# A Perceiver block on one NeuronCore: self-attention's projections placed beside its units, norms batch by batch, biases loaded as columns

## The chip, the cores and the metric

The kernel runs on one NeuronCore of one Trainium2 chip. The metric is the device time of one execution in microseconds (us). Engines: PE is TensorE, DVE is VectorE, ACT is ScalarE, POOL is GpSimd, SP is SyncE, which here only issues DMAs.

## The reference, cut to what matters

Two batches of 256 tokens with 512 features go through three layers. Each layer normalises its input and adds its output to it.

```python
x = x + cross_attention(layernorm(x), ctx)   # 16 heads of 128, 8 key/value heads, 4096 context tokens
n = layernorm(x)                             # self-attention: 16 heads of 32, 256 tokens
Q, K, V = n @ q_w.T + q_b, n @ k_w.T + k_b, n @ v_w.T + v_b
S = K @ Q.T * 32 ** -0.5                     # per batch and head, row i, column j
S = where(i - j < 0, -inf, S) - (i - j)
x = x + (softmax(S) @ V) @ o_w.T + o_b
n = layernorm(x)                             # 8 experts, the best 2 of each token, and a shared one
x = x + routed_experts(n) + 0.2 * shared_expert(n)
```

The projections run in two parts, high and low, of fp32r numbers: each product is three matmuls for each of the four chunks of 128 features, 12 in all for a 128 x 512 result.

## The kernel before, in words

Four stages run one after the other, each a block of five instruction streams (SP, POOL, DVE, ACT, PE) that meet at its end: `queries`, `cross`, `selfattn`, `experts`. A stream is in order. Inside a block semaphores alone order the engines (`wait_ge`, `then_inc`), and the order of the work is written out by hand in each stream. There is no planner. X holds the residual stream, four tiles (TT = 4) of 128 tokens, two (RT = 2) for each batch.

`cross` (L295 to L1119) walks over both batches and 8 key/value heads (a `group` each). In a group PE makes keys and scores into a ring of four PSUM banks (`free`, L986), DVE takes each block of scores out and its maximum (`scores_out`, L823), `maxima` (L830) makes the bias of the exponentials, and ACT computes them (`exp_piece`, L633). The first group of batch 1 (`op` and not `pv`, L926) also adds the last output of batch 0 to X (`residual`, L842) and otherwise makes only keys and scores. In the last group of all, the weights of self-attention are loaded in the order q, k, v, and POOL splits those of q and k (`weight_part`, L116).

`selfattn` (L1122) starts with `ln_vector` (L64) over all four tiles on DVE, with the square root on ACT. PE transposes the result (L1323), ACT copies the high part (L1286), DVE makes the low part (L1214). PE then makes the four chunks of Q and the four of K (L1330); DVE writes Q (L1218), ACT writes K (L1290). Scores of unit 0 follow, then V (L1385), and then the units' loop. A unit n is four heads of one batch: N = 8 units, batch 0 first. In loop n PE issues, in this order: the scores of unit n + 1 (L1340, into the four banks of `s_all`), the transposes of unit n for its first 128 queries (L1353), the values' matmuls of unit n - 1 (L1365), the transposes for the second 128 queries. DVE takes the maxima (`scores`, L1221), makes the reciprocals of the sums (`inverse`, L1234) and copies a part of the turned tiles (`turned`, L1251); ACT does the exponentials (`softmax`, L1292), the other copies (`turned`, L1299) and the high part of the output (`output_high`, L1303); POOL multiplies by the reciprocals (`normalise`, L1197). ACT's order in loop n is softmax(n + 1, 0), turned(n, 0), output_high(n - 1), softmax(n + 1, 1), turned(n, 1). Loop 7 has no scores; in their place stand the output projections of the first two tiles (`out`, L1369), those of batch 1 end the stage. The turned tiles have three PSUM banks, one for each transpose group of a unit.

`experts` (L1405) begins with `ln_vector` (L1602) and the transposes of its result (L1850), which ACT copies twice (L1747, L1748). The biases b1, b2, sb1 are loaded as rows, turned by two transposes (L1853, L1854) and copied by DVE (L1609, L1610). Then come the gate (L1859), the shared expert, whose first layer is L1868, and the eight experts. POOL fills constants, scales a bias (L1576) and adds it to X in one instruction (L1579).

## Time and profile before

| | us |
|---|---|
| median of 3 runs (lowest to highest) | 1970.67 (1969.95 to 1971.15) |
| profiled execution, its own time | 1973.03 |
| its span, first to last instruction | 1971.3 |
| mean granted clock of PE | 0.985 of full |

| share of the span | busy us |
|---|---|
| PE | 1906.8 (97%) |
| DVE | 1094.1 (56%) |
| ACT | 975.7 (49%) |
| POOL | 328.3 (17%) |

The profile is one execution. A line of the timeline is: start in us, duration in us, engine, line of the kernel, operation, output<-inputs, shapes, count of instructions merged into the line, and in brackets the idle time before it and what ended it. A line of the windows' view gives busy us (and instructions) of each engine in a stretch, then the clock granted to PE as a share of full speed, then the DMA engines' share and rate. Self-attention runs from 1418 to 1524 us.

### The profile page before, as it was taken

The page shows a single profiled execution, that of the slowest core. Times are in us where ns is not written, and L with a number is a line of the kernel's source. Part 1 is how long each engine was busy: PE and PEld are TensorE (multiplying, and loading weights), DVE is VectorE, ACT ScalarE, POOL GpSimd, SP SyncE. Part 2 cuts the span into 40 slices and gives each one's busy share as a digit, 9 for nine tenths or more (in the row PEclk, how much of TensorE's full clock was granted, in tenths as well). Part 3 has the DMA queues.
Part 4 walks back from the last instruction along what each step waited for, and adds up shares of the span by engine and source line. Part 5 has one row for each costly group of instructions (what it writes and reads, how often), then busy time and mean ns, then how long its engine had stood idle before and what let it go on. Part 6 is the DMA issues. An engine that isn't in the chain of part 4 may idle for free. (4 is left out here: it accounts for less than half of the span.)

```text
span 1971.3 us, 32041 instructions
## 1 busy us (share of the span) xinstructions
PE 1906.8 (97%) x10480; PEld 1602.1 (81%) x10480; DVE 1094.1 (56%) x2429; ACT 975.7 (49%) x2064; POOL 328.3 (17%) x238
## 2 busy tenths in 40 slices
PE   9999999999999999999999999999787999999998
PEld 6787888888888778878888888887565688999997
DVE  3667677677767666676677677676636531000003
ACT  3204676676577572055775776676526442122111
POOL 0300211211211213011211212211533200000001
PEclk9999999999999999999999999999889899999999
DMA  8651111111111146501111111111300907577552
GB/s 246 214 194 42 43 42 41 51 32 50 45 32 37 43 155 196 173 25 46 36 48 40 37 45 40 37 43 57 104 0 14 352 7 265 203 268 265 198 187 66
DMA packets 123073, 198.12 MB, mean 101 GB/s; under 512 B 12485, under 2 KB 61813, under 8 KB 118896
## 3 DMA queue, kind: packets, MB, share of 16 engines
q1 hardware_dynamic: 119040, 188.59, 28.6%
q10 hardware_dynamic: 2672, 4.55, 0.7%
q0 software_dynamic: 1280, 3.93, 0.6%
q8 instruction: 47, 0.77, 0.2%
q14 instruction: 34, 0.28, 0.0%
HBM read 151.50 MB, written 45.81 MB: 100 GB/s over the span
## 5 line engine op out<-in xcount | busy, mean ns | idle before, releaser
L817 DVE TENSOR_TENSOR crs_ptl<-crs_tp,crs_pth 128x512 fp32r<-128x512 f32 x512 | 352.7, 689 | 178.8 <-ACT crs_pth L650 178.2
L650 ACT ACTIVATE crs_pth<-crs_tp 128x512 fp32r<-128x512 f32 x504 | 301.7, 599 | 245.3 <-PE crs_tp L1036 242.2
L568 POOL TENSOR_TENSOR crs_vl<-crs_vraw,crs_vh 128x512 fp32r<-128x512 f32 x128 | 165.1, 1290 | 1068.8 <-ACT crs_vh L657 1068.7
L1027 PE MATMUL crs_ring<-crs_kh,crs_ql 128*128 128x512 f32 x512 | 233.9, 457 | 0.0
L1046 PE MATMUL crs_ov<-crs_ptl,crs_vh 128*128 128x512 f32 x512 | 210.5, 411 | 10.2 <-DVE crs_ptl L817 8.4
L1046 PE MATMUL crs_ov<-crs_pth,crs_vh 128*128 128x512 f32 x512 | 202.4, 395 | 0.0
L1027 PE MATMUL crs_ring<-crs_kh,crs_qh 128*128 128x512 f32 x512 | 201.5, 394 | 0.0
L1027 PE MATMUL crs_ring<-crs_kl,crs_qh 128*128 128x512 f32 x512 | 200.9, 392 | 0.0
L1046 PE MATMUL crs_ov<-crs_pth,crs_vl 128*128 128x512 f32 x512 | 200.7, 392 | 0.0
L1036 PEld LDWEIGHTS crs_tp<-all_ident,crs_prob 128*128 128x128 f32 x1024 | 142.4, 140 | 69.5 <-ACT crs_more L639 3.7
L639 ACT ACTIVATE crs_prob<-crs_prob,crs_nmax 128x512 f32<-128x512 f32 (+1 forms) x192 | 166.3, 867 | 65.3 <-DVE crs_nmax L832 65.3
L1036 PE MATMUL crs_tp<-all_ident,crs_prob 128*128 128x128 f32 x1024 | 195.2, 272 | 2.8 <-ACT crs_more L639 2.8
L1036 PE MATMUL crs_tp<-all_ident,crs_more 128*128 128x128 f32 x1024 | 195.7, 273 | 0.0
L827 DVE CUSTOM_DVE_ANT_0 crs_more<-crs_ring,crs_maskb 128x512 f32<-128x512 f32 x256 | 172.6, 682 | 0.3 <-issue 0.3
L827 DVE CUSTOM_DVE_ANT_0 crs_prob<-crs_ring,crs_maskb 128x512 f32<-128x512 f32 x256 | 172.6, 683 | 0.0
L639 ACT ACTIVATE crs_more<-crs_more,crs_nmax 128x512 f32<-128x512 f32 (+1 forms) x192 | 166.0, 864 | 0.0
L1721 DVE TENSOR_SCALAR ex_yT<-moe_bank,moe_b_cols 128x160 f32<-128x160 f32 x32 | 10.8, 379 | 273.5 <-PE moe_bank L1992 273.5
L821 DVE TENSOR_TENSOR crs_kl<-crs_ring,crs_kh 128x512 fp32r<-128x512 f32 x128 | 88.4, 691 | 132.5 <-ACT crs_kh L661 132.5
L1808 ACT ACTIVATE ex_hT<-moe_bank,moe_b_cols 128x160 f32<-128x160 f32 x128 | 43.5, 391 | 235.6 <-PE moe_bank L1968 235.6
L1968 PE MATMUL moe_bank<-moe_bufT,moe_w 128*128 128x160 f32 x1024 | 145.4, 302 | 0.7 <-ACT moe_bufT L1803 0.7
L1968 PEld LDWEIGHTS moe_bank<-moe_bufT,moe_w 128*128 128x128 f32 x1024 | 141.5, 192 | 2.8 <-ACT ex_hT L1808 1.0
L1036 PEld LDWEIGHTS crs_tp<-all_ident,crs_more 128*128 128x128 f32 x1024 | 127.6, 140 | 0.0
(279 smaller groups left out, 3334.5 us busy)
## 6 DMA issues: line engine op xcount, KB each, us to landing
moe_w<-in_L_ffn_w SPq DMA_DIRECT2D x48, 1024.0 KB, 12.3
v_scratch<-crs_more SPq DMA_DIRECT2D x64, 512.0 KB, 2.9
crs_vraw<-v_scratch SPq DMA_DIRECT2D x128, 256.0 KB, 2.7
ex_w<-in_L_ffn_w SPq DMA_DIRECT2D x16, 1024.0 KB, 13.4
crs_prob<-in_ctx SPq DMA_DIRECT2D x16, 512.0 KB, 4.7
crs_wo<-in_L_xattn_Wo SPq DMA_DIRECT2D x16, 512.0 KB, 4.1
moe_w<-in_L_ffn_sw SPq DMA_DIRECT2D x8, 1024.0 KB, 12.9
qry_wq<-in_L_xattn_Wq SPq DMA_DIRECT2D x16, 256.0 KB, 3.8
```

What stands on the lines that cost most here:

```text
L568: nc.gpsimd.tensor_tensor(vl[:, n % VR, :, :], vraw[:, :, :], vh[:, n % VR, :, :].bitcast(F32), ALU.subtract).then_inc(s["v_lo"], 1)
L639: act.activation(w, w, ACT.Exp, bias=nmax[:, t:t + 1], accum_out=rs[:, t, PIECE_OF[n]:PIECE_OF[n] + 1]).then_inc(s["p_ready"], 1)
L650: act.activation(pth[:, k % PT, :], tp[k % PT][:, :], ACT.Copy).then_inc(s["pt_hi"], 1)
L817: v.tensor_tensor(ptl[:, k % PT, :], tp[k % PT][:, :], pth[:, k % PT, :].bitcast(F32), ALU.subtract).then_inc(s["pt_lo"], 1)
L821: v.tensor_tensor(kl[:, n % KR, :], ring[k_at(n, op) % RING][:, :], kh[:, n % KR, :].bitcast(F32), ALU.subtract).then_inc(s["ring_free"], 1)
L827: v.tensor_tensor_reduce(probs(t, n * BANK, (n + 1) * BANK), ring[at % RING][:, :], maskb[:, n * BANK:(n + 1) * BANK], op0=ALU.add, op1=AL ...
L1027: m = pe.matmul(ring[at % RING][:, :], a[:, t // RT, rows], w[:, n % KR, :], start=i == 0, stop=i == 2)
L1036: m = pe.transpose(tp[k % PT][:, t * P:(t + 1) * P], probs(t, k * P, (k + 1) * P), ident[:, :])
L1046: m = pe.matmul(ov[:, :], a[:, k // NC % VR, k % NC, :], w[:, k % PT, :], start=k == 0 and i == 0, stop=k == SCH - 1 and i == 2)
L1721: m = v.tensor_scalar(yT[:, c, :], y_ps[c // 2][:, c % 2 * SL:(c % 2 + 1) * SL], b_cols[:, bass.ds(e * KC + c, 1)], None, ALU.add)
L1808: m = act.activation(hT[:, 2 * n + q, :], h_ps[n % 2][:, q * SL:(q + 1) * SL], ACT.Gelu, bias=b1_cols[:, bass.ds(e * FC + (2 * n + q), 1)])
L1968: m = pe.matmul(h_ps[n % 2][:, q * SL:(q + 1) * SL], w1[i][:, c, fc * P:(fc + 1) * P], bufT[:, i, c, :], start=c == 0, stop=c == KC - 1)
```

## The change: what it does

- Layer norm is cut into `ln_variance`, `ln_root`, `ln_deviation` and `ln_scale` for a range of tiles. Statistics and deviation of batch 0 for self-attention are made in the first group of batch 1 of `cross` (on DVE after the residuals of batch 0; the root and two loads of ACT's tables after the keys; the deviation before the last block of scores). Those of batch 0 for the experts are made in the last part of self-attention, after the residuals of batch 0. Batch 1's are made in the stages themselves.
- Self-attention: its weights are loaded and placed in the order v, q, k, so that POOL splits those of v and q in `cross` and those of k in the stage. PE starts with two matmuls on the identity whose result nobody reads, turns batch 0, makes its V, turns batch 1, makes its V, then Q and K of chunk 0 only, and the scores of unit 0. Units alternate between the batches (units 2c and 2c + 1 use chunk c), and the other three chunks of Q and K are made in loops 0 to 4, after the first transposes, the second projection of loop 0 after the second transposes. They use one PSUM bank, `made`; the turned tiles have two banks in place of three, in rotation. DVE writes Q in the loop between the scores and the reciprocal; ACT writes K at the loop's end.
- The first output projection stands after the last unit's transposes, the second after its values.
- Experts: two matmuls on the identity first, transposes batch by batch, POOL's stream waits for the norm before its first fill, and the biases are loaded from arrays turned on the host, without PE and DVE.

```diff
+def ln_variance(v, ch, X, w, start, stop, var_ready):
+    for i in range(start, stop):
+        v.bn_stats(w["stats"][:, i, :], X[:, i, :]).then_inc(ch.sem, 1)
+    ch.n += stop - start
+    v.wait_ge(ch.sem, ch.n)
+    for i in range(start, stop):
+        v.bn_aggr(w["mv"][:, i, :], w["stats"][:, i, :]).then_inc(ch.sem, 1)
+    ch.n += stop - start
+    v.wait_ge(ch.sem, ch.n)
+    v.tensor_scalar(w["veps"][:, start:stop], w["mv"][:, start:stop, 1], EPS, None, ALU.add).then_inc(var_ready, 1)
...
+def ln_deviation(v, ch, w, start, stop, root_ready, count):
+    at = slice(start, stop)
+    v.wait_ge(root_ready, count)
+    ch.link(v.reciprocal(w["div"][:, at], w["root"][:, at]))
+    ch.link(v.tensor_tensor(w["div"][:, at], w["div"][:, at], w["veps"][:, at], ALU.mult))
+    ch.link(v.tensor_tensor(w["div"][:, at], w["div"][:, at], w["root"][:, at], ALU.add))
+    ch.link(v.tensor_scalar(w["div"][:, at], w["div"][:, at], 0.5, None, ALU.mult))
+    ch.link(v.reciprocal(w["rstd"][:, at], w["div"][:, at]))
...
+def ln_scale(v, X, out, w, i, done):
+    m = v.tensor_scalar(out[:, i, :], X[:, i, :], w["mv"][:, i, 0:1], w["rstd"][:, i:i + 1], ALU.subtract, ALU.mult)
+    if done:
+        m.then_inc(done, 1)
...
+                    if op and not pv and n == SB - 3:
+                        act.wait_ge(s["var_ready"], 1)
+                        ln_root(act, norm, 0, RT, s["root_ready"])
+                        act.activation(norm["table"][:, :], ident[:, 0:1], ACT.Exp)
...
+                if op and not pv:
+                    v.wait_ge(s["ring_free"], R + o_at(QT - 1) + 1)
+                    ch = Chain(v, s["ln_chain"])
+                    ln_variance(v, ch, X, norm, 0, RT, s["var_ready"])
...
+                    if op and not pv and n == SB - 2:
+                        ln_deviation(v, ch, norm, 0, RT, s["root_ready"], 1)
...
+    QUERY_BESIDE = {0: 1, 1: 2, 3: 3}
+    KEY_BESIDE = {0: 1, 2: 2, 4: 3}
+    WARM = 2
...
-        bank = [t.ps(f"bank{i}") for i in range(4)]
-        t_ps = (bank[0:1], bank[1:3])
+        turns = [t.ps(f"turn{i}") for i in range(2)]
+        o_bank, made = t.ps("o"), t.ps("made")
+        v_ps = (turns[0], turns[1])
...
+        def t_ps(n, it, j):
+            return turns[(n * BANKS + it + j) % 2]
...
+        def place(n):
+            return n % B * KC + n // B
...
+            def input_low(b):
+                for c in range(KC):
+                    v.wait_ge(s["xT_hi"], b * KC + c + 1)
+                    v.tensor_tensor(xl[:, c, batch(b)], s_all[:, c, batch(b)], xh[:, c, batch(b)].bitcast(F32), ALU.subtract).then_inc(s["xT_lo"], 1)
+            def value(i):
+                v.wait_ge(s["v_ps"], i + 1)
+                v.tensor_tensor(V.rearrange("p (b c) r n -> p b r c n", b=B)[:, i // RT, i % RT], v_ps[i % 2][:, :].rearrange("p (c n) -> p c n", c=KC),
+                                vo_bias[:, 0, :].rearrange("p (c n) -> p c n", c=KC), ALU.add).then_inc(s["v_ok"], 1)
+            def query(c):
+                v.wait_ge(s["q_ps"], c + 1)
+                v.tensor_scalar(qT[:, c, :], made[:, :], bias_cols[:, 0, c:c + 1], HW ** -0.5, ALU.add, ALU.mult).then_inc(s["q_ok"], 1)
+            for i in range(RT):
+                ln_scale(v, X, xn, norm, i, s["xn_ready"] if i == RT - 1 else None)
+            ln_variance(v, ch, X, norm, RT, TT, s["var_ready"])
+            input_low(0)
+            ln_deviation(v, ch, norm, RT, TT, s["root_ready"], 1)
+            for i in range(RT, TT):
+                ln_scale(v, X, xn, norm, i, s["xn_ready"] if i == TT - 1 else None)
+            v.wait_ge(s["vo_ld"], 32)
+            value(0)
+            value(1)
+            input_low(1)
+            value(2)
+            value(3)
             v.wait_ge(s["b_ld"], 32)
-            for c in range(KC):
-                v.wait_ge(s["q_ps"], c + 1)
-                v.tensor_scalar(qT[:, c, :], s_all[:, c, :], bias_cols[:, 0, c:c + 1], HW ** -0.5, ALU.add, ALU.mult).then_inc(s["q_ok"], 1)
+            query(0)
             v.wait_ge(s["consts"], 2)
             def scores(n, it):
...
-                                vo_bias[:, 0, :].rearrange("p (c n) -> p c n", c=KC), ALU.add).then_inc(s["v_ok"], 1)
             for n in range(N):
                 if n < N - 1:
                     scores(n + 1, 0)
+                if n in QUERY_BESIDE:
+                    query(QUERY_BESIDE[n])
                 inverse(n, 1)
...
                     output_low(n - 1)
-            for i in range(RT):
-                residual(i)
+            residual(0)
             output_low(N - 1)
+            residual(1)
+            v.wait_ge(s["out_ok"], RT)
+            ln_variance(v, ch, X, norm_ffn, 0, RT, s["var_ready"])
+            ln_deviation(v, ch, norm_ffn, 0, RT, s["root_ready"], 2)
             for i in range(RT, TT):
...
+            def key(c):
+                act.wait_ge(s["k_ps"], c + 1)
+                act.activation(kT[:, c, :], (made if c else o_bank)[:, :], ACT.Identity, bias=bias_cols[:, 1, c:c + 1]).then_inc(s["k_ok"], 1)
...
+            ln_root(act, norm, RT, TT, s["root_ready"])
+            input_high(1)
+            act.activation(norm["table"][:, :], ident[:, 0:1], ACT.Exp)
             act.wait_ge(s["b_ld"], 32)
-            for c in range(KC):
-                act.wait_ge(s["k_ps"], c + 1)
-                act.activation(kT[:, c, :], bank[c][:, :], ACT.Identity, bias=bias_cols[:, 1, c:c + 1]).then_inc(s["k_ok"], 1)
+            key(0)
...
                     turned(n, it)
                     if n and it == 0:
                         output_high(n - 1)
+                    if it == 1 and n in KEY_BESIDE:
+                        key(KEY_BESIDE[n])
             output_high(N - 1)
+            act.activation(norm_ffn["table"][:, :], ident[:, 0:1], ACT.Sqrt)
+            act.wait_ge(s["var_ready"], 2)
+            ln_root(act, norm_ffn, 0, RT, s["root_ready"])
...
+            def turn_input(b):
+                pe.wait_ge(s["xn_ready"], b + 1)
+                if b:
+                    pe.wait_ge(s["xT_lo"], KC)
+                for c in range(KC):
+                    for i in range(b * RT, (b + 1) * RT):
+                        m = pe.transpose(s_all[:, c, i * P:(i + 1) * P], xn[:, i, c * P:(c + 1) * P], ident[:, :])
+                    m.then_inc(s["xT_ps"], 1)
...
+            def query(c):
+                if c:
+                    pe.wait_ge(s["q_ok"], c)
+                if c > 1:
+                    pe.wait_ge(s["k_ok"], c)
+                project(Q_W, c, made, s["q_ps"])
+            def key(c):
+                if c == 0:
+                    pe.wait_ge(s["w_lo"], 2)
+                else:
+                    pe.wait_ge(s["q_ok"], c + 1)
+                project(K_W, c, made if c else o_bank, s["k_ps"])
             def scores(n, it):
                 if n and it == 0:
...
-                c, b = n % KC, n // KC
+                c, b = n // B, n % B
+                if it == 0:
+                    pe.wait_ge(s["q_ok"], c + 1)
+                    pe.wait_ge(s["k_ok"], c + 1)
...
-                if n:
-                    pe.wait_ge(s["cT_ok"], unit(n - 1, it))
-                    if it == 1:
-                        pe.wait_ge(s["cT2_ok"], n)
                 for j in range(it + 1):
+                    if it + j == 0:
+                        if n:
+                            pe.wait_ge(s["cT_ok"], unit(n - 1, 1))
+                    elif it + j == 1:
+                        if n:
+                            pe.wait_ge(s["cT2_ok"], n)
+                    else:
+                        pe.wait_ge(s["cT_ok"], unit(n, 0))
...
+            for i in range(WARM):
+                pe.matmul(made[:, :].rearrange("p (r n) -> p r n", r=BANK // P), ident[:, :],
+                          ident[:, :].rearrange("p (o n) -> p o n", o=1).to_broadcast([P, BANK // P, P]), start=True, stop=True)
+            turn_input(0)
+            value(0)
+            value(1)
+            turn_input(1)
+            value(2)
+            value(3)
+            query(0)
+            key(0)
+            pe.wait_ge(s["xT_lo"], TT // RT * KC)
             scores(0, 0)
             scores(0, 1)
-            pe.wait_ge(s["w_lo"], 2)
...
             pe.wait_ge(s["v_ok"], TT)
             for n in range(N):
                 for it in range(RT):
-                    if n == N - 1:
-                        out(it)
-                    elif it == 0:
+                    if it == 0 and n < N - 1:
                         scores(n + 1, 0)
                         scores(n + 1, 1)
                     transposes(n, it)
-                    if n and it == 0:
-                        values(n - 1, 0)
-                        values(n - 1, 1)
+                    if it == 0:
+                        if n in QUERY_BESIDE:
+                            query(QUERY_BESIDE[n])
+                        elif n in KEY_BESIDE:
+                            key(KEY_BESIDE[n])
+                        if n:
+                            values(n - 1, 0)
+                            values(n - 1, 1)
+                    elif n in QUERY_BESIDE and n in KEY_BESIDE:
+                        key(KEY_BESIDE[n])
+            out(0)
             values(N - 1, 0)
             values(N - 1, 1)
+            out(1)
             for i in range(RT, TT):
                 out(i)
...
+            pool.wait_ge(s["xn_ready"], B)
             nc.gpsimd.memset(xe[:, :, :, :], 0.0).then_inc(c, 1)
...
-            pool.wait_ge(s["xn_ready"], 1)
...
+            for i in range(RT):
+                ln_scale(v, X, xn, norm, i, s["xn_ready"] if i == RT - 1 else None)
+            ln_variance(v, ch, X, norm, RT, TT, s["var_ready"])
+            ln_deviation(v, ch, norm, RT, TT, s["root_ready"], 1)
+            for i in range(RT, TT):
+                ln_scale(v, X, xn, norm, i, s["xn_ready"] if i == TT - 1 else None)
             for c in range(KC):
...
+            act.activation(norm["table"][:, :], ident[:, 0:1], ACT.Sqrt)
...
+            act.dma_start(b1_cols[:, :], a["L0_ffn_b1"]).then_inc(r, 16)
+            act.dma_start(b_cols[:, 0:SB1], a["L0_ffn_b2"]).then_inc(r, 16)
+            act.dma_start(b_cols[:, SB1:SB1 + FC], a["L0_ffn_sb1"]).then_inc(r, 16)
...
+            ln_root(act, norm, RT, TT, s["root_ready"])
...
+            for i in range(WARM):
+                pe.matmul(bank[7][:, :].rearrange("p (r n) -> p r n", r=BANK // P), ident[:, :],
+                          ident[:, :].rearrange("p (o n) -> p o n", o=1).to_broadcast([P, BANK // P, P]), start=True, stop=True)
+            for b in range(B):
+                pe.wait_ge(s["xn_ready"], b + 1)
+                for c in range(KC):
+                    for i in range(b * RT, (b + 1) * RT):
+                        m = pe.transpose(bank[c][:, i * P:(i + 1) * P], xn[:, i, c * P:(c + 1) * P], ident[:, :])
+                    if b == B - 1:
+                        m.then_inc(s["xT_ps"], 1)
...
+        if name in ("L0_ffn_b1", "L0_ffn_b2", "L0_ffn_sb1"):
+            a = _np.ascontiguousarray(a.reshape(-1, P).T)
```

## Rows read from the trace of the kernel before

**Rows 1.** Windows: stretch and length; PE, PEld, DVE, ACT, POOL busy; PEclk; DMA.
```profile
1418.00:1420.00 2.00, 0.00 (x0) 0.00 (x0) 1.71 (x3) 1.49 (x2) 1.20 (x2) 0.98 0.10 10
1420.00:1422.00 2.00, 0.00 (x0) 0.00 (x0) 1.63 (x9) 0.20 (x1) 0.00 (x0) 0.50 0.80 193
...
1470.00:1472.00 2.00, 0.00 (x0) 0.00 (x0) 1.93 (x10) 1.58 (x9) 1.46 (x1) 0.78 0.00 0
...
1480.00:1500.00 20.00, 14.18 (x215) 9.38 (x215) 17.89 (x93) 19.77 (x78) 10.34 (x9) 1.00 0.01 2
1468.00:1504.60 36.60, 26.12 (x341) 17.77 (x341) 30.17 (x159) 31.97 (x124) 17.13 (x14) 0.91 0.01 2
```

**Rows 2.** Timeline, from the end of cross-attention to the first loop.
```profile
1416.71 0.39 PE L995 MATMUL crs_ring<-crs_woh,crs_pth 128*128 128x512 f32 x1
...
1418.29 2.47 DVE L69 BATCH_NORM_STATS2 att_ln_stats<-all_X 128x6 f32<-128x512 f32 x4 [0.33 <-PEq L358]
...
1422.68 1.92 DVE L85 TENSOR_SCALAR att_xn<-all_X,att_ln_mv,att_ln_rstd 128x512 f32<-128x512 f32 x4
1424.70 3.68 PE L1323 MATMUL att_bank<-all_ident,att_xn 128*128 128x128 f32 x16 [7.60 <-DVEq L1211]
...
1429.79 2.07 PE L1330 MATMUL att_s<-att_xh,all_w_lo 128*128 128x512 f32 x4 [1.41 <-DVE att_xl L1214]
...
1434.41 1.09 PE L1330 MATMUL att_s<-att_xh,all_w_lo 128*128 128x512 f32 x4
...
1455.04 0.94 PE L1340 MATMUL att_s<-att_qT,att_kT 32*128 32x128 f32 x16 [0.87 <-ACT att_kT L1290]
...
1458.74 0.17 DVE L1232 TENSOR_SCALAR att_nmax<-att_mx 128x4 f32<-128x4 f32 x1
...
1468.16 0.94 PE L1340 MATMUL att_s<-att_qT,att_kT 32*128 32x128 f32 x16 [0.78 <-DVE att_V L1261]
```

**Rows 3.** Timeline, one unit of self-attention's loop.
```profile
1484.77 0.94 PE L1340 MATMUL att_s<-att_qT,att_kT 32*128 32x128 f32 x16
...
1487.01 0.64 PE L1365 MATMUL att_bank<-att_cT,att_V 128*32 128x128 f32 x16 [0.36 <-ACT att_cT L1301]
...
1487.15 1.55 POOL L1201 TENSOR_TENSOR att_sc<-att_sc,att_rsum 128x512 f32<-128x512 f32 x1 [1.58 <-DVE att_rsum L1236]
...
1488.75 1.09 PE L1353 MATMUL att_bank<-all_ident,att_sc 128*128 128x128 f32 x8 [1.09 <-POOL att_sc L1201]
...
1489.41 0.51 ACT L1296 ACTIVATE att_sc<-att_sc,att_nmax 128x256 f32<-128x256 f32 x1
...
1489.77 0.94 PE L1340 MATMUL att_s<-att_qT,att_kT 32*128 32x128 f32 x16
...
1491.39 0.57 ACT L1301 ACTIVATE att_cT<-att_bank 128x512 f32<-128x512 f32 x1
```

**Rows 4.** Timeline of PE's weight loads, extra matmuls at the kernel's start.
```profile
8.15 0.19 PEld L271 LDWEIGHTS qry_warm<-all_ident 128*128 128x128 f32 x1 [0.24 <-issue]
8.57 0.19 PEld L271 LDWEIGHTS qry_warm<-all_ident 128*128 128x128 f32 x1 [0.24 <-issue]
```

**Rows 5.** Timeline, last unit of self-attention to the experts' gate.
```profile
1504.60 1.16 PE L1375 MATMUL att_s<-all_w_hi,att_ol 128*128 128x512 f32 x4
...
1524.03 2.47 DVE L69 BATCH_NORM_STATS2 sh_ln_stats<-all_X 128x6 f32<-128x512 f32 x4 [0.32 <-PEq L1131]
...
1535.79 5.37 PE L1859 MATMUL moe_bank<-sh_xnT,moe_gate 128*8 128x512 f32 x8 [1.07 <-ACT sh_xnT L1748]
```

**Rows 6.** Timeline, first group of batch 1 in cross-attention, start and end.
```profile
825.92 2.72 DVE L849 SCALAR_TENSOR_TENSOR all_X<-crs_ring,crs_rinv,all_X 128x512 f32<-128x512 f32 x4
...
829.39 0.69 DVE L821 TENSOR_TENSOR crs_kl<-crs_ring,crs_kh 128x512 fp32r<-128x512 f32 x1 [0.76 <-ACT crs_kh L661]
...
858.44 0.73 ACT L639 ACTIVATE crs_prob<-crs_prob,crs_nmax 128x512 f32<-128x512 f32 x1 [7.85 <-DVE crs_nmax L832]
...
861.42 0.44 PE L1036 MATMUL crs_tp<-all_ident,crs_prob 128*128 128x128 f32 x2 [1.42 <-ACT crs_more L639]
```

124 lines of the change are left out of this document (49 added, 75 removed).

## The prediction

> **What bounds the kernel now.** I read the page first: TensorE (PE) is busy nearly all of the span, so time is lost or won only where PE waits, runs at half clock, or gets more work. Then I cut the span into stretches and looked for PE idle time. From 1400 to 1540 us there is the only long stretch with gaps that the change touches: the end of cross-attention, self-attention and the start of the experts. Behind it PE is full at full clock to the end, so what this stretch gains or loses passes to the end one to one. The small stretches show the granted clock: 0.98 in 1418-1420, though PE's last matmul had ended at 1417.1, 0.50 in 1420-1422; and 0.78 in 1470-1472, in which PE did nothing, three us after the values' projections had kept it full [rows 1, 2]. 0.50 is the lower of the clock's two levels (1.2 GHz), 1.00 the higher (2.4 GHz). Last the timeline, instruction by instruction. At the start of self-attention the norm takes 1418.3 to 1424.7, the transposes of its result run at half clock, eight projections follow, and the first scores come at 1455.04; the values' projection (V) lies behind them, so the units' loop starts with the scores of unit 1 at 1468.16 [rows 2]. A unit then repeats every 5.0 us. Its period is a chain: scores on PE (0.94), the maxima and the reciprocal on DVE (POOL starts 2.38 after the scores), POOL's normalising 1.55, transposes (about 1.0), next scores [rows 3]. ACT is busy 19.77 of 20 us beside it [rows 1]. So the loop is bound by a chain through four engines and by ACT, with PE idle 36.60 - 26.12 = 10.5 us in it [rows 1].
>
> **The change part by part.** I call the stage's start 0 (1418.3) and sum against the profiled execution.
>
> *Start of self-attention.* The statistics of batch 0 are made in cross-attention, so DVE begins with two scalings (0.48 each, a quarter of the old 1.9) and PE has its input at 1.0. PE first runs two extra matmuls, four instructions; at full clock one takes 0.43 (8.15 to 8.57 [rows 4]), so 1.7, and the clock was still full just there [rows 1]. Then 8 transposes: 16 took 3.68 at half clock, so 8 take 0.9 at full; about 1.1 to the first V matmul for ACT's copies (from the end of the old transposes at 1428.4 to the first projection it was 1.4, with twice the columns to copy); V of two tiles. One projection is 2.80: seven from 1434.41 to 1455.04 less 0.9 for the last handover [rows 2]. Then transposes of batch 1 0.9, handover 1.1, V of two tiles, Q0, K0, handover 0.9. Sum: 1.7 + 0.9 + 1.1 + 5.6 + 0.9 + 1.1 + 5.6 + 5.6 + 0.9 = 23.4 to the first scores. DVE's second half of the norm lies beside V0 and V1, POOL's split of the K weights (from about 6.7, 7 long, as before) ends at about 13.7, before K0 at 19.7. Unit 1's scores must wait until DVE has read unit 0's, 3.8 later (1455.04 to 1458.9 [rows 2]); V hid this before, nothing does now. So the loop starts at 27.2 where it started at 49.9: **-22.7**. Six projections (16.8) of that are only moved; 5.9 is norm and half clock.
>
> *Six projections in the units.* Loops 1 and 3 get a query projection, 2 and 4 a key projection, 0 both.
> Query loop: DVE's order is scores of n+1, the query's write, then the reciprocal that POOL waits for. So the chain is scores 0.94, transposes 0.55, Q 2.80, DVE's write with handover 0.95, reciprocal 0.25, POOL 1.6, transposes 0.95: 8.05 in place of 5.0. The projection is wholly on the chain.
> Key loop: the turned tiles now share two banks, so the first transposes of unit n wait for ACT's copy of the unit before (it starts 1.62 and ends 2.19 after the scores: 1491.39 against 1489.77 [rows 3]). Then transposes 0.55 (2.75), K 2.80 (5.55), values 1.0 (6.6; 24 instructions, of which 16 take 0.64 [rows 3]). ACT's queue is in order: its copy of the values' output waits for that, and behind it stand the softmax of the next unit (2.0: 1489.41 to 1491.39), the copy of the turned tile 0.6 and the key's write, 0.7 of the 0.87 that the first scores waited for it [rows 2, 3], for which the next scores wait: 6.6 + 0.5 + 2.0 + 0.6 + 0.7 + handovers 0.3 = 10.7.
> Loop 0: scores, transposes once POOL is done (2.2 after the scores' start), Q 2.8, write and reciprocal 1.2, POOL 1.6, transposes 1.0, K 2.8, write 1.05: 12.65.
> Loops 5 and 6 stay 5.0. Sum 12.65 + 8.05 + 10.7 + 8.05 + 10.7 + 10 = 60.15 against 1504.60 - 1468.16 = 36.4 [rows 2, 5]: **+23.7**. The bounds: PE's 10.5 idle us absorb as much (16.8 - 10.5 = +6.3), or all as above.
>
> *Half clock in the loops.* New gaps on PE: 2.9 before unit 1's scores, 2.8 before loop 0's second transposes, 2.9 at the end of both key loops (while ACT does softmax, copy and key). Both idle stretches of that size in the old trace, at 1418 and at 1470, ended in half clock [rows 1], so I expect most of these to. The first projection before ran 1429.79 to 1434.41, 4.6 in place of 2.8 [rows 2]: 1.8 for a projection, 0.4 for four transposes, 0.7 for scores. First gap 2.2, taken whole; the others 2.75, 3.0 (before loop 3) and 1.6 (loops 5, 6; as much as the old loops 0 to 6 took over seven times 5.0, 36.4 - 35, and a little) are taken at seven tenths: 5.1. **+7.3**; bounds 0 and +9.6.
>
> *End of self-attention.* The first output projection no longer goes ahead of the last unit's transposes. From the loop's end: transposes at 2.25 (ACT's copy), values, transposes 3.75 to 4.75, DVE's write of cT and of the low part until 6.0, then four projections and the last values: 6.1 + 2.8 + 0.9 + 2.8 + 5.5, and the residual 0.9 make 19.0; before it was 19.4 (1504.60 to 1524.03 [rows 5]). PE idles more in it than before, 2.2 and 1.3 us, and half clock on the first of the four projections would cost 1.8: **+1.0** (-0.4 to +1.7). The norm's statistics for the experts, 3.1 on DVE, lie beside the third output projection.
>
> *Start of the experts.* DVE has batch 1's input ready at 5.35 (2 scalings, variance 1.8, root and deviation 1.5, 2 scalings), the last ACT copy then comes at about 10.1, where it came at 11.8 (1535.79). PE idles 2.8 between both batches' transposes, so I leave the gate at half clock. The bias columns come by the same queue and take two transposes off PE, which lay beside ACT anyway. Less a little for POOL's long add, which moves with it: **-1.5**; bounds 0 and -3.3 (clock kept, gate 3.6 in place of 5.4: eight instructions of 0.43, and a tail [rows 4, 5]).
>
> *Statistics in cross-attention.* DVE gets 1.8 us (two statistics of 0.62, a quarter of 2.47 [rows 2], two aggregates, one add) between the residual's end at 828.6 and the split of the third keys at 829.39 [rows 6]. The keys' bank comes free 1.1 later, and PE, which wants it at 830.6, waits 0.7. The deviation (five small operations, 1.0) stands before the last block's scores, at whose end ACT waits 7.85 us for DVE's maximum and PE 1.42 for ACT [rows 6]: all of it counts. ACT's two table loads (3 us with their activations) lie in its idle time. **+1.7**, bounds 0 and +3.
>
> Sum: -22.7 + 23.7 + 7.3 + 1.0 - 1.5 + 1.7 = **+9.5**. The profiled execution took 1973.03 (span 1971.3), so its successor 1982.5; the median of the runs is 2.4 below it, hence 1970.7 + 9.5 = **1980.2**.
>
> **A rule against it.** The 16 transposes at 1424.70 took 0.23 each, and after their 3.7 us of work the first projection still needed 4.6; only the second took 2.8 [rows 2]. Work of that kind did not bring the full clock, so the extra matmuls may not hold it over 0.9 us of transposes and two handovers of 1.1: then the transposes take 0.9 more and the V projections of the first batch 1.8 to 2.8 more, about +3.7, so 1984 (a rival below). The Trainium skill (TensorE: Matmul & The Clock Gate, Part 4: PE-mode transpose) says that transposes do not count as activity in the way that matmuls do; by that rule, the trace agrees.
>
> **The rivals.** *The idle time takes the projections* (0.18). Then the loops grow by 16.8 - 10.5 = 6.3, no gap is long, and the sum is -22.7 + 6.3 - 1.5 + 1.7 = -16: 1954.5. For it: PE idles 10.5 us. Against: the query stands before the reciprocal in DVE's own queue. It decides if a query loop takes under 6 us.
> *The chain grows, the clock stays* (0.20): -22.7 + 23.7 + 0 - 1.5 + 1.7 = +1.2, 1972. For it: the clock was still 0.98 two idle us after 1417.1 [rows 1]. It decides if no 2 us stretch from 1440 to 1500 is under 1.00.
> *The extra matmuls do not hold the clock at the start* (0.10): 1984, worked out above.
> My forecast has 0.52.
>
> **Range and chances.** Within 0.2% (3.9 us) is what a measurement of this kernel cannot tell from no change. Forecast and third rival are slower: 0.62, less 0.02 for sizes below 3.9: 0.60. The second is same: 0.20. The first is faster: 0.20 with the rest. The unknown sizes (cross 0 to 3, half clock 0 to 9.6, experts 0 to -3.3) put my own case at 1973 to 1985; with the second rival and a part of the first the range is 1966 to 1986.
>
> **What would show it.** Right: first scores about 23.4 us after self-attention's start; query loops near 8 and key loops near 10.7; POOL waiting for the reciprocal, ACT's values copy waiting for PE; granted clock below 1.00 near the start of the loops; DVE's nmax one us or more later in the group at 858. Wrong: query loops under 6 (then the first rival); scores of unit 1 not 3.8 behind unit 0; full clock all through.

## The result and the profile after

The changed kernel took 1979.19 us (median of 5 runs, 1978.39 to 1981.44), the kernel before 1970.67 beside it: a ratio of 1.0047 (95% interval 1.0033 to 1.0062). It is slower by 8.5 us; 1980.2 was forecast. Run again later it was 1.0039 (1.0025 to 1.0053), so the experiments are set against 1.0043. The profiled execution of the changed kernel is its fastest run (1978.39, span 1976.7); that of the kernel before (1973.03) lies above all five of its runs here (1969.95 to 1971.15). So between the two traces only 5.4 us are to be found.

First the stretches of the changed kernel's trace, cut where the prediction cut them: self-attention's start to the first scores, loops 0 to 6 (each from its unit's scores to the next), the tail behind them, the start of the experts. Columns as in [rows 1]; the last but two is the granted clock.

```profile
1420.06:1442.94 22.88, 20.57 (x93) 15.90 (x93) 11.15 (x27) 6.15 (x14) 17.16 (x12) 1.00 0.20 70
1446.96:1462.38 15.42, 11.99 (x53) 9.22 (x53) 5.23 (x25) 7.59 (x29) 3.63 (x3) 0.71 0.00 1
1462.38:1470.92 8.54, 6.78 (x65) 5.08 (x65) 4.26 (x22) 3.57 (x15) 2.48 (x2) 0.91 0.00 0
1470.92:1480.58 9.66, 7.00 (x66) 5.13 (x65) 5.54 (x25) 7.04 (x26) 2.70 (x3) 0.90 0.01 2
1480.58:1488.42 7.84, 6.08 (x64) 4.55 (x64) 4.25 (x22) 2.88 (x11) 1.78 (x2) 1.00 0.00 1
1488.42:1498.61 10.19, 6.13 (x65) 4.58 (x65) 5.50 (x25) 7.73 (x29) 3.39 (x3) 1.00 0.01 2
1498.61:1504.46 5.85, 4.81 (x53) 3.53 (x53) 3.50 (x21) 3.62 (x15) 2.59 (x2) 0.63 0.00 0
1504.46:1510.20 5.74, 4.52 (x53) 3.08 (x52) 4.52 (x23) 4.08 (x16) 1.80 (x2) 0.78 0.01 3
1510.20:1532.12 21.92, 17.51 (x109) 13.32 (x109) 8.62 (x21) 5.86 (x17) 2.34 (x2) 0.84 0.00 1
1532.12:1546.62 14.50, 9.21 (x28) 3.42 (x28) 7.84 (x19) 7.34 (x14) 6.92 (x9) 0.76 0.93 293
```

The seven loops are now 63.2 us for 36.4 before; a query loop (1 and 3) is about 8, a key loop (2 and 4) about 10, and loop 0 has one projection of each kind. Next, how a query loop is held, in the timeline of loop 3 (scores at 1480.58, answering to [rows 3]).

```profile
1483.78 1.07 PE L1447 MATMUL att_made<-att_xl,all_w_hi 128*128 128x512 f32 x4
1484.88 0.75 DVE L1292 TENSOR_SCALAR att_qT<-att_made,att_bias_cols 128x512 f32<-128x512 f32 x1 [2.12 <-PE att_made L1447]
1485.55 0.17 DVE L1326 RECIPROCAL att_rsum<-att_rsum 128x4 f32<-128x4 f32 x1
1485.80 1.55 POOL L1270 TENSOR_TENSOR att_sc<-att_sc,att_rsum 128x512 f32<-128x512 f32 x1 [8.35 <-DVE att_rsum L1326]
1487.40 1.09 PE L1492 MATMUL att_turn<-all_ident,att_sc 128*128 128x128 f32 x8 [1.76 <-POOL att_sc L1270]
```

DVE waits 2.12 us for PE with the query's write at the head of its queue. The reciprocal behind it needs nothing from PE, but POOL waits for it (8.35 us idle), and PE's transposes wait for POOL (1.76 us). A key loop is held on ACT; here are PE and ACT at the end of loop 4, without the softmax's four operations from 1495.35 to 1497.4.

```profile
1493.07 1.07 PE L1447 MATMUL att_made<-att_xl,all_w_hi 128*128 128x512 f32 x4
...
1494.06 0.86 PE L1504 MATMUL att_o<-att_cT,att_V 128*32 128x128 f32 x24
...
1495.07 0.39 ACT L1403 ACTIVATE att_oh<-att_o 128x256 fp32r<-128x256 f32 x1 [2.25 <-PE att_o L1504]
...
1497.32 0.58 ACT L1399 ACTIVATE att_cT<-att_turn 128x512 f32<-128x512 f32 x1
1497.79 0.67 ACT L1380 ACTIVATE att_kT<-att_made,att_bias_cols 128x512 f32<-128x512 f32 x1
...
1498.61 0.72 PE L1474 MATMUL att_s<-att_qT,att_kT 32*128 32x128 f32 x12 [2.66 <-ACT att_kT L1380]
```

The key is ready on PE at 1494.1 and its write starts 3.7 us later, behind the output's copy, a softmax and another copy. ACT had idled 2.25 us ahead of the output's copy, which needs the values, and PE makes the values only behind the key's projection. The last view of this kernel is PE at the tail (the first output projection) and at the start of the experts.

```profile
1513.88 1.97 PE L1492 MATMUL att_turn<-all_ident,att_sc 128*128 128x128 f32 x8
1516.96 2.07 PE L1514 MATMUL att_s<-all_w_hi,att_ol 128*128 128x512 f32 x4 [1.11 <-DVE att_ol L1334]
1518.83 1.91 PE L1514 MATMUL att_s<-all_w_lo,att_oh 128*128 128x512 f32 x4
...
1541.68 5.01 PE L2018 MATMUL moe_bank<-sh_xnT,moe_gate 128*8 128x512 f32 x8 [3.10 <-ACT sh_xnT L1905]
1546.62 1.20 PE L2027 MATMUL moe_bank<-sh_xTh,sh_s1l 128*128 128x512 f32 x4
```

The last transposes (1.97 for eight), the first output projection (2.07, 1.91) and the gate run at half clock. The kernel before had a fall of the clock in its tail too, on the first output projection of batch 1:

```profile
1515.74 2.08 PE L1375 MATMUL att_s<-all_w_hi,att_ol 128*128 128x512 f32 x4 [1.01 <-DVE att_ol L1244]
1517.62 1.69 PE L1375 MATMUL att_s<-all_w_lo,att_oh 128*128 128x512 f32 x4
```

### The profile page after: what moved, and what is told of

Read it like the earlier page. It is cut to its first block and busy times, and to the rows that moved or that the text cites. A ratio compares the mean times of both kernels' runs of the same rounds, so it can differ in the third digit from the quotient of the medians.

```text
span 1976.7 us, 32080 instructions
## 1 busy us (share of the span) xinstructions
PE 1909.9 (97%) x10486; PEld 1602.1 (81%) x10486; DVE 1095.7 (55%) x2443; ACT 979.2 (50%) x2075; POOL 328.9 (17%) x238
## 5 line engine op out<-in xcount | busy, mean ns | idle before, releaser
L870 DVE CUSTOM_DVE_ANT_0 crs_more<-crs_ring,crs_maskb 128x512 f32<-128x512 f32 x256 | 172.7, 682 | 0.0
```

Of the source, the lines that this page charges most:

```text
L870: v.tensor_tensor_reduce(probs(t, n * BANK, (n + 1) * BANK), ring[at % RING][:, :], maskb[:, n * BANK:(n + 1) * BANK], op0=ALU.add, op1=AL ...
```

## The experiments

Two measures stand beside each other. One is the ratio to the kernel before, which was run again beside each group of experiments. The other is the length of "the stretch", from VectorE's first operation of self-attention to the experts' first layer. It is read from one trace each, and one fall of the clock moves it by up to 3 us. It is 122.8 us before, 126.6 in the changed kernel and 126.2 in its second profile.

| run | what it is | ratio (95%) | stretch |
|---|---|---|---|
| c1 | changed kernel again | 1.0039 (1.0025-1.0053) | 126.2 |
| e1 | all projections in front | 0.9987 (0.9978-0.9997) | 115.9 |
| e2 | query's write later | 0.9996 (0.9987-1.0005) | 119.5 |
| e3 | key's write one place sooner | 1.0034 (1.0020-1.0048) | 128.7 |
| e4 | first gap filled | 1.0025 (1.0016-1.0034) | 123.6 |
| e5 | key's write ahead of the output's copy | 1.0004 (0.9994-1.0014) | 119.6 |
| e6 | statistics back out of cross-attention | 1.0055 (1.0042-1.0068) | 129.9 |
| e7 | old start of the experts | 1.0050 (1.0035-1.0065) | 129.2 |
| e8 | e2 and e5 together | 0.9968 (0.9953-0.9983) | 112.8 |
| e9 | no extra matmuls in self-attention | 1.0047 (1.0031-1.0063) | 127.1 |
| b1 | projections behind first scores | 0.9971 (0.9958-0.9983) | 111.3 |
| b2 | b1 and filled gaps at the gate | 0.9951 (0.9937-0.9966) | 111.1 |

**Is it where the projections stand?** (e1)

```diff
-    QUERY_BESIDE = {0: 1, 1: 2, 3: 3}
-    KEY_BESIDE = {0: 1, 2: 2, 4: 3}
+    QUERY_BESIDE, KEY_BESIDE = {}, {}
...
-            query(0)
-            key(0)
+            for c in range(KC):
+                query(c)
+                key(c)
...
```

> The changed kernel with all eight query and key projections made before the first scores, none in the units' loop. Theory of the prediction (in the loop each projection is paid as the chain that it lengthens, 26.8 us for six in the changed kernel's trace, against 16.3 in front, 6 x 2.72): the loops go from 63.2 us back to about 40 (36.4 before, and the first unit's chain no longer lies behind the values), the first scores move from 22.9 to 39.2 after the stage's start, together -7: 1972 (1969 to 1975). Rival (a projection costs its own matmuls wherever it stands): 1979, no change.

The ratio fell by 0.0056, 11 us, and the stretch by 10.6. The first scores came 38.2 after the stage's start, loop 0 was 6.55 at half clock, loop 1 5.74, then 5.02 each. The rival, that a projection costs its matmuls wherever it stands, fell: with the queues in this order, a projection in the loop costs more than its matmuls.

**Which chain holds a query loop?** (e2)

```diff
-                if n in QUERY_BESIDE:
-                    query(QUERY_BESIDE[n])
                 inverse(n, 1)
                 if n < N - 1:
                     scores(n + 1, 1)
                     inverse(n + 1, 0)
+                if n in QUERY_BESIDE:
+                    query(QUERY_BESIDE[n])
```

> The changed kernel with one move on VectorE: the write of a query projection stands behind the next unit's inverse instead of ahead of this unit's. Theory (a query loop is a chain through VectorE's queue, which waits there for TensorE's projection): the loops with a query, 8.54 and 7.84 us and part of the first, fall by about 1.5 us each: 1975 (1974 to 1976.5). Rival (TensorE's own work sets these loops, 3.7 busy of an old loop and 2.7 for the projection, with the half clock): 1979, no change.

It brought more than either theory said: 0.0047 of the ratio (9 us), 7 us of the stretch. VectorE and GpSimd in loop 1, then loops 0 to 2:

```profile
1461.12 0.69 DVE L1330 TENSOR_TENSOR att_sc<-att_sc,att_rsum 128x512 f32<-128x512 f32 x1
1461.17 1.55 POOL L1270 TENSOR_TENSOR att_sc<-att_sc,att_rsum 128x512 f32<-128x512 f32 x1 [7.30 <-DVE att_rsum L1326]
...
1463.39 0.72 DVE L1292 TENSOR_SCALAR att_qT<-att_made,att_bias_cols 128x512 f32<-128x512 f32 x1
```

```profile
1447.37:1458.82 11.45, 10.58 (x53) 8.01 (x53) 5.22 (x25) 7.59 (x29) 3.62 (x3) 0.77 0.01 1
1458.82:1464.85 6.03, 6.03 (x64) 4.55 (x64) 4.14 (x22) 2.93 (x13) 2.59 (x2) 1.00 0.00 0
1464.85:1474.85 10.00, 6.12 (x65) 4.58 (x65) 5.50 (x25) 7.55 (x28) 2.59 (x2) 1.00 0.01 2
```

POOL starts 2.35 after the scores, as in a unit of the kernel before, and the projection runs beside it. PE is busy through the whole query loop, 6.03 of 6.03: 1.0 longer than an old unit for 2.7 us of matmuls. So 1.8 us of each query loop hung on the place of one write (7.84 to 6.03, both at full clock). Of loop 0 it was 2.4 to 4.0: 11.45 here at a clock of 0.77, against 15.42 at 0.71 and 13.86 at 0.82 in the two profiles of the changed kernel.

**Which chain holds a key loop?** (e3, e5) The wait named in the trace is the key's write, and ACT's queue offers two places to mend it.

```diff
                     if n < N - 1:
                         softmax(n + 1, it)
+                    if it == 1 and n and n in KEY_BESIDE:
+                        key(KEY_BESIDE[n])
                     turned(n, it)
                     if n and it == 0:
                         output_high(n - 1)
-                    if it == 1 and n in KEY_BESIDE:
+                    if it == 1 and n == 0 and n in KEY_BESIDE:
                         key(KEY_BESIDE[n])
```

> The changed kernel with one move on ScalarE: the key projection's write of the third and fifth unit stands ahead of the copy of the turned probabilities instead of behind it. TensorE waited 2.66 us for that write at the start of two units' scores. Theory (ScalarE's order is what makes these loops 9.66 and 10.19 us): about -2 each, 1975 (1974 to 1976.5). Rival (the next wait, for GpSimd's or VectorE's part of the normalising, stands right behind it): 1979, within 1 us.

It took 0.5 off a key loop (10.19 to 9.71), and PE still waited at the scores behind loop 4:

```profile
1498.73 0.94 PE L1476 MATMUL att_s<-att_qT,att_kT 32*128 32x128 f32 x16 [2.18 <-ACT att_kT L1380]
```

The rest is lost in the spread: this trace's stretch is longer than the changed kernel's because the clock was down in loop 3 (9.33 for 7.84) and through the whole gate (6.54 for 5.01). The write had been put past one copy, but the output's copy and the softmax of 2.0 us still stood ahead of it.

```diff
                     turned(n, it)
+                    if it == 0 and n and n in KEY_BESIDE:
+                        key(KEY_BESIDE[n])
                     if n and it == 0:
                         output_high(n - 1)
-                    if it == 1 and n in KEY_BESIDE:
+                    if it == 1 and n == 0:
                         key(KEY_BESIDE[n])
```

> The changed kernel with one move on ScalarE: in the third and fifth loop the key's write stands ahead of the output's copy and of the second tile's softmax. In the changed kernel's trace ScalarE idled 2.25 us in front of the output's copy (TensorE made the values only behind the 2.7 us projection), then came 2.5 us of softmax, the turned copy and the key, and TensorE's next scores waited 2.66 us for the key. Theory (it is ScalarE's order from the output's copy on, not that of the last two writes): the next scores no longer wait, the key loops fall from 9.7 and 10.2 to 7.3 to 8.2: -4 to -5 against the changed kernel. Rival (the delay of ScalarE's softmax comes back in the next loop): within 1 us.

The end of loop 4 of this kernel, PE and ACT:

```profile
1492.86 0.69 ACT L1380 ACTIVATE att_kT<-att_made,att_bias_cols 128x512 f32<-128x512 f32 x1 [1.34 <-PE att_made L1449]
1493.55 1.09 PE L1494 MATMUL att_turn<-all_ident,att_sc 128*128 128x128 f32 x8
1493.76 0.39 ACT L1403 ACTIVATE att_oh<-att_o 128x256 fp32r<-128x256 f32 x1 [0.21 <-PE att_o L1506]
1494.57 0.72 PE L1476 MATMUL att_s<-att_qT,att_kT 32*128 32x128 f32 x12
```

The scores wait for nothing, the key loops are 6.82 and 7.44, 2.8 less each. The query loop between them got 1.3 longer (9.10 for 7.84): its first transposes wait 1.22 us for ACT's copy of the last turned tile, which now ends later. The ratio fell by 0.0039, the stretch by 7 us. The write now fills a part of ACT's idle time, and the softmax ends as long after the loop's scores as it did (its first exponential starts 6.9 us behind them in both traces). This edit moved the write past the output's copy and the softmax at once; a write between the two was not tried, so which of them it had to pass is open.

**Do the two add up?** (e8: both edits above)

> The changed kernel with both moves together: VectorE's query write behind the next unit's inverse, ScalarE's key write ahead of the output's copy; all six projections stay beside the units. Theory (each move took its own wait away, 6.0 us for a query loop and 6.8 to 7.4 for a key loop): the sum of both, -12 against the changed kernel, ratio to the kernel before 0.998. Rival (both free the same time, or the clock falls at the fuller loops again): -7 to -8, no better than the first move alone.

Very nearly: 0.0075 of the ratio, where the single moves brought 0.0047 and 0.0039, and 13.8 us of the stretch, where they brought 7 each. That is more than the 12 expected. Its loops 0, 1, 2 and 5 (3 and 4 are 7.29 as well):

```profile
1447.07:1458.55 11.48, 10.61 (x52) 8.05 (x53) 5.22 (x25) 7.59 (x29) 3.62 (x3) 0.77 0.01 1
1458.55:1464.56 6.01, 6.01 (x65) 4.56 (x65) 4.13 (x22) 2.94 (x13) 2.59 (x2) 1.00 0.00 0
1464.56:1471.85 7.29, 6.07 (x66) 4.55 (x65) 4.47 (x23) 5.64 (x22) 2.59 (x2) 1.00 0.01 2
...
1486.43:1491.46 5.03, 3.41 (x54) 2.39 (x53) 4.47 (x23) 4.79 (x19) 1.81 (x2) 1.00 0.00 0
```

With both writes moved, the kernel with its projections beside the units is faster than the kernel before (0.9968): the change lost by the order of two writes, not by its idea. How much the place beside the units is worth can be read from the time between self-attention's start and the end of loop 6, one trace each: 76.3 us here, 79.5 with all projections in front (e1), 86.3 in the kernel before, 90.1 in the changed one.

**What does the clock cost?** (e4, c1)

```diff
             scores(0, 1)
 
+            for i in range(3):
+                pe.matmul(made[:, :]..., ident[:, :], ident[:, :]..., start=True, stop=True)
             pe.wait_ge(s["v_ok"], TT)
```

> The changed kernel with three more matmuls of the identity on TensorE (2.9 us at the full clock) between the first unit's scores and the second's, where it idled 3.0 us and the granted clock fell to 0.50; their result is read by nobody. Theory (the idle time ahead of the loop lowers the clock, and this made the first loop 15.4 us instead of 12.65): -2.2 to -2.8, 1976.5. Rival (the first loop is set by the chain through VectorE, ScalarE and GpSimd, or the clock falls at the next gap anyway): 1979, within 0.7 us.

> The changed kernel itself once more, as the measure of the runs beside it: 1.0047 of the kernel before. If the loops and the clock are what its first runs showed, the units' loops take 63 us again; if the places at which the clock falls are chance, some loops differ by 2 to 3 us.

Loops 0 to 5 of the filled kernel, then of the changed kernel's second profile:

```profile
1447.05:1459.30 12.25, 8.17 (x53) 6.14 (x53) 5.22 (x25) 7.59 (x29) 3.62 (x3) 1.00 0.00 1
1459.30:1467.17 7.87, 6.11 (x64) 4.55 (x64) 4.26 (x22) 2.88 (x11) 1.78 (x2) 1.00 0.00 0
1467.17:1477.35 10.18, 6.12 (x65) 4.58 (x65) 5.50 (x25) 7.72 (x29) 3.39 (x3) 0.97 0.01 2
1477.35:1488.11 10.76, 9.00 (x65) 6.66 (x65) 4.25 (x22) 2.87 (x11) 1.79 (x2) 0.71 0.00 1
1488.11:1498.30 10.19, 6.13 (x66) 4.58 (x65) 5.50 (x25) 7.72 (x29) 3.38 (x3) 1.00 0.01 2
1498.30:1503.29 4.99, 3.36 (x52) 2.38 (x53) 3.50 (x21) 2.77 (x11) 1.80 (x2) 1.00 0.00 0
```

```profile
1448.95:1462.81 13.86, 10.44 (x53) 7.81 (x53) 5.23 (x25) 7.58 (x29) 3.63 (x3) 0.82 0.00 1
1462.81:1470.68 7.87, 6.11 (x64) 4.55 (x65) 4.25 (x22) 2.88 (x11) 1.78 (x2) 1.00 0.00 0
1470.68:1483.12 12.44, 8.84 (x65) 6.48 (x65) 5.54 (x25) 7.72 (x29) 3.39 (x3) 0.73 0.01 1
1483.12:1492.55 9.43, 7.66 (x65) 5.70 (x65) 4.25 (x22) 2.88 (x11) 1.78 (x2) 0.82 0.00 1
```

Filling the gap gave loop 0 back 3.2 us (15.42 to 12.25), and loop 3 lost 2.9 (7.84 to 10.76), where the clock had stayed full without the filling. The stretch won 2.9. In the second profile of the same program loops 2 and 3 cost 2.8 and 1.6 more than in the first, loops 0 and 1 1.6 and 0.7 less. So the same gaps were followed by a lower clock at one place in one execution and at another in the next, and a fall cost up to 3 us where it came. Against the loops at full clock (12.25, 7.87, 10.18, 7.84, 10.19, 4.99), loops 0 to 5 lost 4.2 us in the first profile and 5.5 in the second.

**The rest of the change.** Self-attention's first statistics back home (e6), the old start of the experts (e7), and self-attention without its two extra matmuls (e9):

```diff
-                if op and not pv:
-                    v.wait_ge(s["ring_free"], R + o_at(QT - 1) + 1)
-                    ch = Chain(v, s["ln_chain"])
-                    ln_variance(v, ch, X, norm, 0, RT, s["var_ready"])
...
+            ln_variance(v, ch, X, norm, 0, RT, s["var_ready"])
+            ln_deviation(v, ch, norm, 0, RT, s["root_ready"], 1)
...
```

> The changed kernel with the first batch's statistics and deviation of self-attention's norm back at the start of self-attention, none of them in the cross-attention. Theory (in the cross-attention's group they cost 1.5 us, as the shift between the two traces grew from 1.7 to 3.2 there; at the stage's start they cost some 3.1, two statistics, the root and five small links): +1.6 against the changed kernel. Rival 1 (the 1.5 us in the group is no cost, the later groups absorb it): +3.1. Rival 2 (they stand beside the table load anyway): -1.5.

In the cross-attention the maxima of two groups, the changed one between them, are 174.3 us apart in the changed kernel (687.2 to 861.5), 174.4 in its second profile, 172.7 in e6 and 172.3 before. So the statistics cost about 1.7 there (the other runs that have them there took 173.9 to 174.4). The later groups do not absorb it: from the second of the maxima to self-attention's start it is 558.6 us in the changed kernel and 558.5 in the kernel before, if the 1.6 that the latter lost by half clock in its last output projections are taken off. In e6 the first scores came 28.1 after the stage's start and not 22.9. Only 2.4 of these 5.2 us are the norm itself, less than the 3.1 expected. The other 2.8 are half clock on the values' projections of batch 0, which took 8.4 for 5.6:

```profile
1430.00:1432.00 2.00, 2.00 (x6) 1.53 (x5) 1.80 (x8) 0.00 (x0) 0.00 (x0) 0.50 0.08 31
```

The stretch rose by 3.5 us for the 1.7 saved (some of the 5.2 came back, since loop 0 lost less to the clock here). So by these traces moving the statistics out was right, but without the clock it was worth only 2.4 for 1.7. The ratio (+0.0012, with intervals that overlap) does not show it.

```diff
...
-            ln_variance(v, ch, X, norm, RT, TT, s["var_ready"])
-            ln_deviation(v, ch, norm, RT, TT, s["root_ready"], 1)
+            ln_variance(v, ch, X, norm, 0, TT, s["var_ready"])
+            ln_deviation(v, ch, norm, 0, TT, s["root_ready"], 1)
...
-    WARM = 2
+    WARM = 0
```

> The changed kernel with the start of the experts' stage as it was: the whole norm at its start, nothing of it in self-attention, no extra matmuls; the biases stay columns. Theory (the changed start is 14.5 us against 17.1 in the traces): +2.6, less what the columns alone bring, 1981 to 1982. Rival (the gate runs at half the clock in both, GpSimd's addition ends last): within 1 us.

From PE's last output projection to the first layer: 18.1 before, 15.5 changed, 18.2 here. So by these traces the norm and its extra matmuls brought 2.7, and the biases as columns, which this run keeps, nothing. The ratio (+0.0007) is too coarse for it.

```diff
-    WARM = 2
+    WARM = 0
```

> The changed kernel without the two extra matmuls of the identity at the start of self-attention. Theory (they keep the granted clock at full until the transposes): the clock falls within the first transposes and values, as it was at 0.50 from 1420 to 1433 in the kernel before, and the start of 22.9 us grows by 2 to 4: 1982. Rival (the stage's gap of 1.2 us ahead of them is too short to lose the clock): within 1 us, and less than the 1.95 us that they take where the norm is ready sooner.

Here is PE's stretch after the cross-attention's last matmul at 1421.2 in this kernel:

```profile
1424.00:1426.00 2.00, 1.59 (x8) 1.19 (x8) 1.93 (x8) 1.37 (x5) 0.00 (x0) 0.63 0.82 165
1426.00:1428.00 2.00, 1.86 (x5) 1.51 (x6) 1.83 (x10) 0.17 (x2) 0.00 (x0) 0.52 1.05 385
```

The clock falls within the transposes, as the theory says, but it is back at 1428 and the first scores come 24.0 after the stage's start, 1.1 later and not 2 to 4. The ratios cannot tell that from nothing.

**A version that beats both the kernel before and the changed one.** (b1, b2) In b1 the projections stand in front, the later ones where they hide the first unit's softmax, and the old order of units and outputs is back (only the first of these moves is shown). In b2, further matmuls of the identity stand in the two gaps ahead of the gate.

```diff
+            query(0)
+            key(0)
             scores(0, 0)
             scores(0, 1)
+            value(2)
+            value(3)
+            for c in range(1, KC):
+                query(c)
+                key(c)
...
```

> The changed kernel with all projections ahead of the loop, the second batch's values and the last six projections behind the first unit's scores, so that they hide that unit's softmax and leave no gap in front of the second scores, and with the units one batch after the other as in the kernel before, so that the first two outputs are made in the last loop. Theory (chain and clock): second scores at 40 us after the stage's start (22.9 + 16.3 + little), no half clock there, loops 36, the end of the stage as before: -13 against the changed kernel, -5 to -8 against the kernel before. Rival (the idle time in front of the second scores was free and the half clock comes at another place): -9 against the changed kernel, no better than with all projections in front.

```diff
                     if b == B - 1:
                         m.then_inc(s["xT_ps"], 1)
+                for i in range(2 + b):
+                    pe.matmul(bank[7][:, :]..., ident[:, :], ident[:, :]..., start=True, stop=True)
```

> The kernel with the projections behind the first scores (0.9971 of the kernel before), and beside it two more matmuls of the identity behind the first batch's transposes of the experts' stage and three behind the second's, 4.9 us of work in idle time of 2.2 and 3.5 us. Theory (the gate's eight matmuls take 5.0 to 5.3 us because the clock is at 0.50): the gate falls to 2.7, -2 to -2.6 more, ratio 0.9959. Rival (GpSimd's addition to X or ScalarE's rounding ends last): no change.

b1 is 0.9971 of the kernel before, some 14 us under the changed kernel. Its interval and that of e8 (0.9968) nearly coincide, so which of the two is faster is open. By the traces b1 reaches the end of loop 6 later (78.4 us after the stage's start for 76.3), and makes up for it behind that: its tail, to the experts' first matmul, is 18.1 us for 21.9, at full clock throughout. Its moves were not tried apart. The second scores come at 41.9 and not 40, and the clock fell all the same (0.50 at 1466 to 1470, loops 5.85 and 5.75, then 5.03). In b2 the gate looks like this:

```profile
1523.40 2.74 PE L2021 MATMUL moe_bank<-all_ident 128*128 128x512 f32 x6
1527.02 3.60 PE L2027 MATMUL moe_bank<-sh_xnT,moe_gate 128*8 128x512 f32 x8 [0.88 <-ACT sh_xnT L1911]
```

The gate takes 3.60 at full clock, 5.25 in b1. From the experts' first matmul to the first layer that is 13.65 for 14.75, 1.1 less and not 2 to 2.6, since the second transposes and the gate begin a little later. The ratio, 0.9951, is the lowest of all, 9.6 us under the kernel before; that b2 is faster than b1 is not shown by the intervals, which overlap.

## Why the prediction was right

*Start of self-attention.* Said 23.4 to the first scores and 27.2 to the second; measured 22.9 and 26.9, -23.0 for -22.7. The third rival (1984) is out: the clock was 1.00 from 1420 to 1442.9, through the extra matmuls, twice eight transposes and two handovers of 0.65 and 0.74 (a handover is the time that the next engine waits for a result). The Trainium skill (TensorE: Matmul & The Clock Gate, Part 4: PE-mode transpose) says that transposes do not count as activity as matmuls do; the trace neither bears that out nor contradicts it, since the transposes and the handover behind them lasted only 1.7 and 1.8 us, with matmuls on both sides. The rival's price for a lost clock was 2.7 to 3.7. Where the clock did fall, it was 1.1 in e9 and 2.8 in e6, so the price was not wrong, but depends on how long the clock stays down.

*Projections in the units.* Said 12.65, 8.05, 10.7, 8.05, 10.7, 5, 5; at full clock (e4's loops for 0, 1, 2, and 4 to 6, loop 3 of the first profile) they are 12.25, 7.87, 10.18, 7.84, 10.19, 5, 5: 58.3 for 60.15, so +21.9 where I had +23.7. The chains are those that were named, each undone by moving one instruction: e2 for VectorE's queue, e5 for ScalarE's. In a key loop the terms came one by one as summed: the key projection was ready 5.7 after the scores (said 5.55), the values at 6.5 (6.6), the softmax done at 9.0 and the next scores at 10.19 (10.7). e3 shows that the order of the last two terms is worth only 0.5; what has to be passed lies ahead of them, the softmax or the output's copy. What I had missed is the size of the other side: with the query's write out of the way a query loop costs 6.0, so the first rival's mechanism is real (its "under 6 us" all but met) and was shut out by two places in two queues.

*Half clock in the loops.* Said +7.3 of 0 to 9.6. For loops 0 to 5 it was 4.2 and 5.5 in two profiles, with loop 6 4.9 in the first. The first gap fell as said. Of the two key loops' gaps one was followed by a fall in each profile (0.54 at 1500 to 1502 in the first; 1484 to 1488 in the second). So the term was 2.4 too high: the gaps did lower the clock, but less often, or over less work, than was put in. It also rested on two idle stretches of the old trace "of that size", of which one (from 1417.1 on) lasted 7.6 us and the clock had fallen about 3 us into it. The second rival (clock stays) is out. The sums of the first two rivals leave out the tail's term, which moves neither by more than 1 us.

*End of self-attention.* Said +1.0, measured +2.5 (21.9 for 19.4 [rows 5]). The case "half clock on the first projection", priced at 1.8, came true (2.07 and 1.91 for 1.2 and 1.1), and the last transposes were slow too (1.97 for 1.1), together some 2.6 us. But the 19.4 that it is held against has half clock in it as well: 2.08 and 1.69 at 1515.74, some 1.4 us, which the prediction did not take off. So of the +2.5 about 1.2 is clock, and the rest the new order of the outputs. In this tail the clock fell in both profiles of the changed kernel and in all of e1 to e9. Of the three kernels with the old order, it fell in the one before and not in b1 and b2. The new order, with 1.5 to 2.3 us of idle time ahead of the last unit's transposes that the old one has not, makes the fall likelier, which belonged in the sum; the old order does not rule it out.

*Start of the experts.* Said -1.5, measured -2.6 (14.5 for 17.1): the gate began 9.6 after the stage's start, said 10.1, and before it was 11.8. The gate stayed at half clock as said. The columns are worth nothing (e7), as said.

*Cross-attention.* Said +1.7; 2.0 by the maxima against the kernel before, 1.6 to 1.7 against e6. Between the two traces the shift at self-attention's start is 1.8 as well, but by chance: 1.3 of it had come before any changed instruction (687.2 for 685.9), and about 1.5 was won at the end, where the last output projections of the cross-attention ran partly at half clock in the trace before and not in this one; in c1 they did again.

The sum by traces: 1.8 - 23.0 + 26.8 + 2.5 - 2.6 = +5.5, against +9.5 forecast; by medians +8.5 and, in the second measurement, 0.39%, 7.7. The time came out nearer than the traces because the profiled execution before lay 2.4 above its median and the changed one 0.8 below. Terms off by up to 4 us (loops with clock, 31.0 for 26.8) were partly balanced by the tail. So the mechanism and the sign were right, the closeness of 1 us is luck.

## What to carry to other kernels

Work put into another engine's idle time costs what waits behind its hand-over: look for the instruction that takes the new result off the engine, and put it in that engine's queue at the last place where it is not late (here 14 us between two orders of the same work). A wait named in the trace is the last link: follow the queue of the engine that is waited for back to its own first idle time, and try the write there (here ahead of a copy that had idled 2.25 us and of a softmax of 2.0). Idle gaps of 2 to 3 us on TensorE were a gamble for up to 3 us each here, so a difference of one stretch between two profiles is worth nothing unless the clock beside it is the same.

## What was not expected of the hardware

One program, two profiles, the same gaps: the clock was 0.71, 0.91, 0.90, 1.00 in loops 0 to 3 of one and 0.82, 1.00, 0.73, 0.82 of the other. In the first, PE's idle time of 2.66 us up to 1480.58 left the clock at 1.00 for the next 18 us; in e4 the same gap, up to 1477.35, was followed at once by half clock, which cost loop 3 2.9 us. Filling one gap moved the loss in part, and removed only the rest. Even shorter gaps showed both: in the tail of the kernel before, idle times of 1.21 and 1.01 us were followed by half clock at 1515.74, and the same two idle times in b1 and b2 left the clock at 1.00. Such falls also touch code that is the same in both kernels: at the cross-attention's last output projections 1.6 us. They may be part of why single runs of the kernel before spread from 1967.7 to 1977.7 us in the later measurements; that was not tried.
